# Moving one small matrix product of a pipelined attention loop to another place in TensorE's order

## The reference

```python
q_hk = (hidden_q @ Wq.T).reshape(Bv, Sv, H, K)
q_big = jnp.einsum('bshk,hkq->bshq', q_hk, w_kc_q)
q_big = _apply_rope(q_big, sin_q, cos_q)          # rotation over the 192 columns
kv_r = _apply_rope(kv_c, sin_k, cos_k)
q_r = jnp.einsum('bshq,hqr->bhsr', q_big, W_qr)
k_r = jnp.einsum('bld,hdr->bhlr', kv_r, W_kr)
scores = jnp.einsum('bhsr,bhlr->bhsl', q_r, k_r)
attn = jax.nn.softmax(scores, axis=-1)
ctx_c = jnp.einsum('bhsl,bld->bhsd', attn, kv_r)
ctx_lat = jnp.einsum('bhsd,hkd->bhsk', ctx_c, w_kc_kv)
ctx = ctx_lat.transpose(0, 2, 1, 3).reshape(Bv, Sv, H * K)
return ctx @ Wo.T
```

## Time and profile before

| what | value |
|---|---|
| three runs, median (lowest to highest) | 413.5 us (413.28 to 413.62) |
| span of the profiled execution | 411.3 us, 6289 instructions |
| the profiled execution's own time | not told apart from the runs; the span is 2.2 us under their median |
| PE busy | 386.1 us (94%), 2121 matmul rows |
| PEld busy | 257.6 us (63%) |
| DVE busy | 306.3 us (74%) |
| ACT busy | 216.8 us (53%) |
| POOL busy | 180.6 us (44%) |
| own-head product L1418 | 64 rows, 17.3 us with overlaps counted once |
| mean granted TensorE clock | 0.988 |

### The profile page before, as it was taken

One profiled execution on the slowest core, in us unless ns is written; L12 is line 12 of the kernel. 1 busy time (PEld: TensorE's weight loads), 2 busy tenths in 40 slices (PEclk: granted clock), 3 DMA queues, 4 the chain that ended last, 5 costly groups with the idle time before them and its releaser, 6 DMA issues.

```text
span 411.3 us, 6289 instructions
## 1 busy us (share of the span) xinstructions
PE 386.1 (94%) x2121; PEld 257.6 (63%) x2121; DVE 306.3 (74%) x676; ACT 216.8 (53%) x579; POOL 180.6 (44%) x170
## 2 busy tenths in 40 slices
PE   8799899999999999999999999988879988999996
PEld 8675556656666666566655677764245445678886
DVE  5796777877767668776668766646989998898673
ACT  1523655555465657556553876327879532574140
POOL 2554456555646554664656422386530042053200
PEclk9999999999999999999999999999977999999999
DMA  7638001020020030000210000300000000000001
GB/s 254 202 125 328 1 22 81 1 104 2 2 102 2 0 104 1 2 0 0 81 63 0 2 0 0 114 0 2 0 1 0 2 0 0 2 1 2 26 27 52
DMA packets 9087, 17.54 MB, mean 43 GB/s; under 512 B 2144, under 2 KB 6944, under 8 KB 8160
## 3 DMA queue, kind: packets, MB, share of 16 engines
q1 hardware_dynamic: 9056, 17.14, 12.4%
HBM read 16.09 MB, written 1.05 MB: 42 GB/s over the span
## 4 chain that ended last, share of the span: by engine, by line
PE 61%; DVE 22%; ACT 9%; issue 4%; DMA 2%; POOL 1%; SPq 0%; DVEq 0%; ACTq 0%
PE bank L1340 7%; PE bank L1464 7%; PE bank L1458 6%; PE bank L1433 6%; PE bank L1342 6%; PE bank L1341 6%; PE bank L1446 5%; DVE rot_up L891 4%; PE bank L1418 3%; ACT prob L629 3%; PE bank L1363 3%; DVE relu L1050 2%; ACT probT L620 2%; PE bank L1412 2%; DMA blobs<-in_blob 2%
## 5 line engine op out<-in xcount | busy, mean ns | idle before, releaser
L462 POOL TENSOR_TENSOR prob<-prob,rinv 128x512 f32<-128x512 f32 x64 | 67.0, 1048 | 106.5 <-DVE rinv L956 106.5
L629 ACT ACTIVATE prob<-bank,negmax 128x256 f32<-128x256 f32 x128 | 60.1, 480 | 39.8 <-DVE negmax L951 39.8
L951 DVE TENSOR_REDUCE negmax<-bank 128x2 f32<-128x512 f32 x64 | 41.2, 686 | 25.1 <-PE bank L1433 24.6
L620 ACT COPY probT<-bank 128x512 f32<-128x512 f32 x64 | 37.8, 591 | 19.2 <-PE bank L1446 19.0
L457 POOL TENSOR_TENSOR rot_low<-rot_low,rot_up 128x512 f32<-128x512 f32 x32 | 40.8, 1276 | 10.9 <-DVE rot_up L891 10.9
L891 DVE TENSOR_TENSOR rot_up<-bank,cb 64x512 f32<-64x512 f32 x64 | 44.1, 689 | 0.9
L1340 PE MATMUL bank<-xnT,w 128*128 128x512 f32 x96 | 42.0, 437 | 2.2 <-DVE xnT L867 1.7
L1446 PEld LDWEIGHTS bank<-ca,prob 128*128 128x128 f32 x256 | 30.5, 141 | 18.8 <-issue 16.1
L889 DVE TENSOR_TENSOR rot_low<-bank,cb 128x512 f32<-128x512 f32 x32 | 22.0, 688 | 25.2 <-PE bank L1342 25.1
L1446 PE MATMUL bank<-ca,prob 128*128 128x128 f32 x256 | 38.9, 275 | 1.8 <-ACT probT L620 1.1
L442 POOL TENSOR_TENSOR c_y<-c_ve,minus_half 128x4 f32<-128x4 f32 (+1 forms) x9 | 9.8, 1087 | 64.9 <-DVE c_ve L848 52.1
(11 more groups left out here) (213 smaller groups left out, 788.3 us busy)
## 6 DMA issues: line engine op xcount, KB each, us to landing
blobs<-in_blob SPq DMA_DIRECT2D x7, 1024.0 KB, 4.9
xs<-in_x SPq DMA_DIRECT2D x2, 512.0 KB, 4.1
xn<-in_w_fc_t SPq DMA_DIRECT2D x1, 1024.0 KB, 4.8
ctxT<-in_w_proj_t SPq DMA_DIRECT2D x1, 1024.0 KB, 5.5
out<-qk SPq DMA_DIRECT2D x8, 128.0 KB, 1.8
cb<-in_const_b SPq DMA_DIRECT2D x1, 768.0 KB, 8.5
blobs<-in_w_gate SPq DMA_DIRECT2D x1, 704.0 KB, 4.3
blobs<-in_w_up SPq DMA_DIRECT2D x1, 704.0 KB, 5.7
```

The source lines that it names most:

```text
L462: pool.tensor_tensor(p[:], p[:], rinv[:, n % PROBS, :].unsqueeze(2).to_broadcast([P, 2, S]), ALU.mult).then_inc(normed, 1)
L620: act.copy(probT[n % 2][:].rearrange("p a s -> p (a s)"), pT[:]).then_inc(probsT_copied, 1)
L629: ins = act.activation(prob[n % PROBS][:, st, :], pS[n % 2][:, st * S:(st + 1) * S], ACT.Exp, bias=negmax[:, n % 2, st:st + 1], accum_out= ...
L951: dve.tensor_reduce(negmax[:, n % 2, :], pS[n % 2][:].rearrange("p (a s) -> p a s", a=2), AX, ALU.max, negate=True).then_inc(max_ready, 1)
```

## The change

The own-head product is issued at the third step of a group, behind that step's context, and no longer at the second, between the transposes of the first step and the fold. The waits that it issues (`joined`, `wqk_ready`, `u_copied`) go with it. The shared product stays at the fourth step.

```diff
+OWN_AT = 2
...
-                if s % 2 == 1 and m // RT - 1 < GROUPS:
-                    n = m // RT - 1
-                    if m % RT < 2:
-                        latent_u(n, m % RT)
+                if s % 2 == 1 and m % RT == 1 and m // RT - 1 < GROUPS:
+                    latent_u(m // RT - 1, 1)
...
                     context(batch_at(s))
+                if s % STEP == OWN_AT and s // STEP - 1 < GROUPS:
+                    latent_u(s // STEP - 1, 0)
                 if unit_at(s - TURN_AFTER) is not None:
```

## The result

| | kernel before | changed kernel |
|---|---|---|
| median of the runs beside each other | 413.39 us (413.0 to 413.62, 4 runs) | 422.69 us (420.22 to 423.16, 4 runs) |
| ratio | | 1.0185, 95% interval 1.0135 to 1.0236 |
| five further runs of the changed kernel, 13 of the kernel before beside them | 413.10 us (412.02 to 415.88) | 420.67 us (420.24 to 421.54), ratio 1.0193, 1.0175 to 1.0212 |
| profiled span | 411.3 us | 418.4 us (of the run of 420.22) |
| start to first scores | 32.38 | 32.10 |

What follows compares the result with a forecast made beforehand. TensorE was taken to bound the loop, with VectorE's rotation limiting the second query product. Terms summed to +7.6 us on the 411.3 us span, 418.9, plus 2.2 from span to run time: 421.1 us (418.4 to 423.9).

Steps and rivals of the forecast that it cites:

- The floor: Between a group's two query products: the second can start no earlier than 0.06 us behind VectorE's rotation of the first.
- Only the slack comes back: Gap between query products: of 1.11 us removed, only 0.29 (L1363 fold) or 0.18 (L1370 fold) returns, nothing in the last pair.
- The price behind the context: At the product's new place, sharing the context's tile shape: scores come 0.86 us later per group.
- The maxima: VectorE's maxima (L951), second half of a group: 1.16 us behind the scores instead of 1.22, so only 0.80 us later.
- The sum: Over 15 places: +2.6 and +3.7 us in groups with folds, +1.6 last pair, 0 first group, -0.25 group 15; +7.6 us.
- group 15: Last group, among output projections and with no query product: TensorE alone sets the pace, -0.25 us.
- The first group of the loop: Its maxima are held by the rotation, so a scores delay up to 1.07 us vanishes: 0 added.
- The span: Whole profiled kernel: 411.3 us plus the added time gives 418.9 us.
- The clock: Rival, behind the loop: TensorE's clock fall lands on other work as that comes 7.6 us later; about 423.5 us, chance 0.08.
- The shape alone: Rival, gap between query products: rotation not limiting, fewer shape changes gain 3.7 us, giving 409.8 us; chance 0.03.
- prices paid again: Rival, behind the context: shape-change prices not shared and maxima give nothing back, 2.7 us more, 423.8 us; chance 0.12.
- absorption in the second half: Rival, second half of a group: the transposes' 0.22 us lateness absorbs 2.9 us, leaving +4.7, 418.2 us; chance 0.11.

Runs made afterwards that it cites:

- the extra product: Changed kernel with the own-head product also issued at its old place as an overwritten spare: 424.38 us, ratio 1.0275 to the kernel before.
- the shortened rotation: One L892 multiplication left out of each group's first query-product rotation (groups 2 on), in both kernels: changed 411.88 us, before 411.28 us.
- The late uT copy: ScalarE's uT copy moved from a group's fourth step to its sixth, in both kernels: before 409.68 us, changed 418.41 us.
- The 66 single matmuls: Kernel before with 66 small matmuls of ones added behind the loop, ahead of the last projection: 427.14 us.

## Why the prediction was right, point by point

The forecast was 421.1 us (418.4 to 423.9), with a range of its own of 419.8 to 422.5; the first four runs gave 422.69, just above that, all nine 421.41. The points below are read from the trace of the run of 420.22, the fastest of the first four. Its mechanism is shown; the 2.4 to 2.9 us that the other three runs took on top are not, and that the medians fell so near to the forecast is in part luck. The 2.2 us added to the span were 0.3 to 0.5 too many, too: wherever a run's time and span stand side by side, they are 1.7 to 1.9 apart.

- *The floor.* 0.06 us behind the rotation, in all 14 groups of the loop that have a second query product: shown by the rows, and the waits view names rot_up 14 times.
- *Only the slack comes back.* 2.65 - 2.35 = 0.30 us measured, 0.29 forecast. Shown by the extra product, which cost 3.5 us for 16.7 us of work, and by the shortened rotation, which took the cost from 8.01 to 0.27.
- *The price behind the context.* 1.88 - 1.02 = 0.86, as forecast, with the shape shared.
- *The maxima.* 159.17 - 158.01 = 1.16 us behind the scores, as forecast, so 0.80 and not 0.86 per group. The late uT copy speaks for it: without that chain the change costs 0.9 us more, of which 0.2 belong to the first group, and 13 x 0.06 is 0.8.
- *The sum.* Without group 15 it was 2.6 + 3.7 + 1.6 = 7.9 us up to the projections; measured 8.01. Term by term, from one group's first scores to the next's: 0.51 to 0.52 in each of the five groups with the fold of L1363 (0.51 forecast), 0.62 to 0.71 in the six with that of L1370 (0.62), 0.79 and 0.75 in the last pair (0.80). The projections: -0.25 forecast, -0.34 measured. The first group of the loop: 0; from its first scores to the next group's it takes 46.38 - 32.38 = 14.00 before and 46.09 - 32.10 = 13.99 after.
- *The span.* 418.9 forecast, 418.4 measured; the 0.5 us lie before and behind the loop (32.38 to 32.10 and 134.68 to 134.41), where nothing was changed.
- *The clock.* The fall is there again. The stretch of low clock in the changed kernel's trace (columns as above), and a wait just ahead of it:

```profile
312.40:322.40 10.00, 10.00 (x29) 5.71 (x28) 9.34 (x10) 10.00 (x10) 0.00 (x0) 0.50 0.00 0
```

```profile
309.77 0.33 PE L1561 MATMUL bank<-ca,pad 128*128 128x128 f32 x1 [2.04 <-DVE pad L1055]
```

  The rival's premise, that the work moves under a fall which keeps its time since the start, did not come true. In all 14 traces taken here a fall begins 25.6 to 28.6 us after the first matmul behind the loop, though that matmul starts anywhere from 271.7 to 313.8 us: 303.3 - 276.65 = 26.7 us after it before the change, 312.3 - 284.02 = 28.3 with it. So the fall goes with the work, to within 3 us: it comes near that wait of about 2 us for VectorE, from 0.2 us before its end to 2.8 behind it. And the part behind the loop takes 134.41 us against 134.68. So in the profiled run this rival had no price; what added 2.4 to 2.9 us to the three other runs is not shown, and only one of them (423.16, at 0.976) goes with a lower clock, as told above.
- *The other rivals.* The shape alone (409.8) is ruled out by the waits; prices paid again, by the 0.86; absorption in the second half, by the transposes, which moved with the scores (4.02 us behind them, 4.07 before).

## What to carry to other kernels

A small product between two uses of one buffer may be the cover of another engine's work on that buffer. Before it is moved, measure the gap from the end of the first use to the start of the second against that engine's chain, and against every other chain that ends in the gap (here ScalarE's copy between two sets of transposes): only the difference can be won, and at its new place the product is paid in full. A saving in TensorE's own time (fewer changes of shape) counts only where TensorE waits for nobody; look first for a wait that another engine's chain ends, as ScalarE's here, and try each order of the copies in that chain (the late uT copy gained 3.66 us).

## What the runs showed of the hardware that was not expected

A fold in the 64-column tile shape behind another product of that shape took 0.53 us for its two pairs of 256 columns, as 0.22 and 0.32 for the one before the shape changes would make (0.54). So the 0.10 us for leaving the shape, read from the context block, is found at another product, and a product that shares its neighbour's shape saves it. The 66 single matmuls of 128 x 128 by 128 float32 columns took 0.21 us each by the medians, where I had put 0.11. The trace agrees: they run from 295.20 to 311.83 at a granted clock of 0.85, which is 0.25 us each, or 0.21 at the full clock. They leave 132 rows, two each, where a transpose of the same size leaves one and takes 0.43 / 4 = 0.11 us.
